# Output projection in two halves of three fp32r matmuls, query projections in parts, and low parts made on GpSimd

## What is computed

```
qn = layernorm(x, ln_q_g, ln_q_b)
q = qn @ Wq * scale                                   # 256x1024 for each batch
k, v = split(media @ Wkv)
sim = where(media_mask, q k^T, lowest);  attn = softmax(sim)
out = attn @ v                                        # 16 heads of 64 = 1024 columns
x = x + tanh(attn_gate) * (out @ Wo)                  # the output projection, Wo is 1024x256
x = x + tanh(ff_gate) * (gelu(layernorm(x) @ W1) @ W2)
... second layer: scores against media, softmax, context, gate, rmsnorm
```

## Time and profile before

| | |
|---|---|
| median of 3 runs | 854.41 us (853.79 to 854.54) |
| the profiled execution | 853.74 us, of which 851.9 us is the span from first to last instruction |
| TensorE busy | 821.6 us, 96% of the span |
| VectorE, ScalarE, GpSimd busy | 616.6, 466.6 and 420.4 us |
| mean granted TensorE clock | 0.996 of full speed |
| DMA | 16.81 MB, under a tenth of the time of the queues after the first slices |

### The profile page before, as it was taken

The page is one execution under the profiler, slowest core; times in us unless marked ns, Lnnn a source line. Parts: engine busy times, 40 slices in busy tenths (PEclk is TensorE's granted clock), DMA queues, the critical chain, the costliest instruction groups (busy, mean ns, idle before and its releaser), DMA issues.

```text
span 851.9 us, 18557 instructions
## 1 busy us (share of the span) xinstructions
PE 821.6 (96%) x7905; PEld 696.2 (82%) x7905; DVE 616.6 (72%) x996; ACT 466.6 (55%) x743; POOL 420.4 (49%) x205
## 2 busy tenths in 40 slices
PE   4999999999999999999999999999999989999996
PEld 3787888888888888888888888888888868998885
DVE  7856789867757898678478986784888766446385
ACT  5755665657536656576266565663555563126262
POOL 2445565655625656556355565564767686000002
PEclk9999999999999999999999999999999999999999
DMA  8100001000000010000000000000100502000001
GB/s 283 31 2 2 2 2 40 2 2 2 2 1 2 1 40 2 2 2 2 1 1 2 2 2 2 2 2 2 50 2 2 156 16 76 3 2 1 1 1 49
DMA packets 20560, 16.81 MB, mean 20 GB/s; under 512 B 1008, under 2 KB 19456, under 8 KB 20480
## 3 DMA queue, kind: packets, MB, share of 16 engines
q1 hardware_dynamic: 20192, 15.38, 6.1%
q10 hardware_dynamic: 288, 0.27, 0.1%
HBM read 14.59 MB, written 1.05 MB: 18 GB/s over the span
## 4 chain that ended last, share of the span: by engine, by line
PE 81%; DVE 11%; ACT 4%; POOL 2%; issue 1%; DMA 1%; ACTq 0%; POOLq 0%; DVEq 0%
PE psum L1396 22%; PE psum L382 18%; PE psum L1410 16%; PE psum L1365 7%; PE psum L1321 4%; PE psum L1425 3%; PE psum L1178 3%; PE psum L1260 2%; DVE mx L983 2%; DVE k_lo L972 2%; DVE ot L1013 2%; PE psum L1416 1%; ACT v L666 1%; POOL acc L495 1%; ACT k_hi L660 1%
## 5 line engine op out<-in xcount | busy, mean ns | idle before, releaser
L495 POOL TENSOR_TENSOR acc<-acc,ring 128x1024 f32<-128x1024 f32 x128 | 306.7, 2396 | 18.7 <-POOL acc L490 0.5
L983 DVE TENSOR_REDUCE mx<-psum 128x2 f32<-128x800 f32 (+2 forms) x256 | 245.3, 990 | 80.9 <-PE psum L1365 68.9
L683 ACT ACTIVATE ring<-psum 128x1024 f32<-128x1024 f32 x192 | 196.8, 1026 | 65.0 <-PE psum L1396 58.6
L490 POOL TENSOR_TENSOR acc<-ring 128x1024 f32<-128x1024 f32 x32 | 76.6, 2394 | 250.2 <-ACT ring L683 250.2
L1410 PE MATMUL psum<-ring,v 128*64 128x256 f32 (+1 forms) x1664 | 186.7, 381 | 1.8
L1410 PEld LDWEIGHTS psum<-ring,v 128*64 128x64 f32 (+1 forms) x1664 | 116.7, 137 | 60.6 <-DVE k_lo L972 3.9
L1396 PE MATMUL psum<-nm,maskrow 64*128 64x256 f32 (+1 forms) x832 | 124.4, 294 | 0.6 <-ACT ring L683 0.6
L1396 PE MATMUL psum<-q_hi,k_hi 64*128 64x256 f32 (+1 forms) x832 | 117.8, 278 | 0.0
L1396 PE MATMUL psum<-q_lo,k_hi 64*128 64x256 f32 (+1 forms) x832 | 117.6, 277 | 0.0
L1396 PE MATMUL psum<-q_hi,k_lo 64*128 64x256 f32 (+1 forms) x832 | 117.4, 277 | 0.0
L675 ACT COPY od<-psum 128x512 f32<-128x512 f32 x32 | 18.8, 587 | 153.2 <-PE psum L1416 153.2
(11 more groups left out here) (165 smaller groups left out, 1478.2 us busy)
## 6 DMA issues: line engine op xcount, KB each, us to landing
nat<-in_ctx_dram SPq DMA_DIRECT2D x7, 768.0 KB
w<-in_L_xattn_W_dram SPq DMA_DIRECT2D x2, 1024.0 KB, 6.4
wo<-in_L_xattn_Wo_dram SPq DMA_DIRECT2D x1, 1024.0 KB, 9.7
out_dram<-t_res SPq DMA_DIRECT2D x8, 128.0 KB, 1.7
mask<-in_mask_BxS_bk_dram SPq DMA_DIRECT2D x4, 200.1 KB, 7.0
nat<-in_ctx_dram SPq DMA_DIRECT2D x2, 384.0 KB, 7.4
ring<-in_L_xattn_Wkv_dram SPq DMA_DIRECT2D x2, 384.0 KB, 6.2
wq<-in_L_xattn_Wq_dram SPq DMA_DIRECT2D x1, 768.0 KB, 6.7
```

What stands on the lines that cost most here:

```text
L490: nc.gpsimd.tensor_tensor(acc[:, :, :, :], ring[:, 0, :, :, :], ring[:, 1, :, :, :], ALU.add)\
L495: nc.gpsimd.tensor_tensor(acc[:, :, :, :], acc[:, :, :, :], ring[:, g, :, :, :], ALU.add)\
L683: nc.scalar.activation(ring[:, g, :, :, :], score_set[m % 2].rearrange("p (h i q) -> p h i q", h=2, i=2), ACT.Exp).then_inc(S["p_ready"], 1)
L983: nc.vector.tensor_reduce(mx[:, t, :, c], pair[:, :, 0:min(c1, KEYS) - c0], axis=AX.X, op=ALU.max).then_inc(S["m_max"], 1)
```

## The change

1. The output projection O becomes two items, `("O", b, 0)` for pairs 0 to 3 and `("O", b, 1)` for pairs 4 to 7. The first stands in stage 5, the second where O stood. Each of its 8 products is three fp32r matmuls (high by high, high by low, low by high). H is also two items. The second H adds to what the first wrote.
2. `F` multiplies in place into `rec` (`ot_made`); a new item f on ScalarE rounds it to `ot_hi`, and GpSimd subtracts to get `ot_lo` (`output_lo`), which raises `ot_ready`. `rec` and `nm` now lie in parts of `ring` that the last group of keys leaves unused.
3. GpSimd splits `Wo` behind its sums of pairs 0 and 1 of batch 0, and `Wq` behind those of pairs 2 and 3.
4. From batch 1 on, G is three fp32r matmuls for each product, on `wq_hi`, `wq_lo`, `zt_hi`, `zt_lo`. A new item a (stage 5) makes `zt_hi` on ScalarE and `zt_lo` on VectorE.
5. `mt_lo` of the next batch moves from VectorE (item P) to GpSimd (`next_media_lo`, behind the sums of pair 5). Two of the four Y move from stage 4 to stage 5.
6. The mask has one buffer instead of four and is loaded by SyncE for each batch; `unread` is gone.

```diff
-FULL_EXTRAS = {2: "G.3 Q.3", 3: "T.1.0 T.1.1 T.1.2", 4: "T.1.3 T.1.4", 5: "W.1", 6: "G.4 Q.4", 7: "G.5 Q.5", 9: "O.0 H.0 G.6 Q.6"}
-COLUMN_EXTRAS = {2: "B.1 J.1", 3: "c.1.0 c.1.1 c.1.2 X.1", 4: "c.1.3 c.1.4 Z.1 C.1 Y.1.0 Y.1.1 Y.1.2 Y.1.3", 5: "P.1.0 P.1.1 P.1.2 P.1.3", 7: "I.1.0 I.1.1"}
+FULL_EXTRAS = {2: "G.3 Q.3", 3: "T.1.0 T.1.1 T.1.2", 4: "T.1.3 T.1.4", 5: "O.0.0 H.0.0 W.1", 6: "G.4 Q.4", 7: "G.5 Q.5", 9: "O.0.1 H.0.1 G.6 Q.6"}
+COLUMN_EXTRAS = {2: "B.1 J.1", 3: "c.1.0 c.1.1 c.1.2 X.1", 4: "c.1.3 c.1.4 Z.1 C.1 Y.1.0 Y.1.1", 5: "a.1 Y.1.2 Y.1.3 P.1.0 P.1.1 P.1.2 P.1.3", 7: "I.1.0 I.1.1"}
...
-    return [("U", j)] + items(COLUMN_EXTRAS.get(j, "")) + [("A", j), ("D", j)]
+    return [("U", j), ("f", j - 1)] + items(COLUMN_EXTRAS.get(j, "")) + [("A", j), ("D", j)]
...
-                n += 2 if item[0] == "M" else 1
+                n += 2 if item[0] == "M" else ABANKS if item == ("O", 0, 0) else 1
...
+            def output_lo(b, n):
+
+                upto(pool, "ot_hi", b, n + 1)
+                nc.gpsimd.tensor_tensor(ot_lo[:, n % HALF, :], rec, ot_hi[:, n % HALF, :].bitcast(F32), ALU.subtract)\
+                    .then_inc(S["ot_ready"], 1)
...
+            def next_media_lo(b):
+
+                upto(pool, "mt_mixed", b, 2 * NCH)
+                for c, (c0, c1) in enumerate(REAL_CHUNKS):
+                    upto(pool, "mt_hi", b, NCH + c + 1)
+                    nc.gpsimd.tensor_tensor(mt_lo[:, c0:c1], mt[:, c0:c1], mt_hi[:, c0:c1].bitcast(F32), ALU.subtract)\
+                        .then_inc(S["mt_lo"], 1)
...
+                    if b or j:
+                        upto(pool, "acc_ready", b, j + 1)
+                        output_lo(b, j - 1)
+                    if b == 0 and j < 2:
+                        upto(pool, "acc_ready", b, j + 1)
+                        split_output_weights((2 * j, 2 * j + 1))
+                    if b == 0 and j in (2, 3):
+                        upto(pool, "acc_ready", b, j + 1)
+                        split_query_weights((0, 1) if j == 2 else (2, 3))
+                    if next_batch and j == 5:
+                        next_media_lo(b)
...
             sums(BATCH - 1, False)
+            output_lo(BATCH - 1, PAIRS - 1)
...
+            def output_hi(b, n):
+
+                upto(act, "ot_made", b, n + 1)
+                if n >= HALF:
+                    upto(act, "o_full", b, n // HALF)
+                nc.scalar.copy(ot_hi[:, n % HALF, :], rec).then_inc(S["ot_hi"], 1)
...
                     elif kind == "F":
                         upto(dve, "rec_ready", b, (n + 1) * RECIPROCAL_PARTS)
-                        if n == PAIRS:
-                            upto(dve, "o_full", b, 1)
-                        nc.vector.tensor_tensor(ot[:, n % PAIRS, :], od[:, 0:TOK], rec[:, :], ALU.mult)\
-                            .then_inc(S["ot_ready"], 1)
+                        nc.vector.tensor_tensor(rec, od[:, 0:TOK], rec, ALU.mult).then_inc(S["ot_made"], 1)
...
+                            parts = [(w[:, t, c], z_t[:, t, :]) for t in range(DT)
+                                     for w, z_t in (((wq_hi, zt_hi), (wq_lo, zt_hi), (wq_hi, zt_lo)) if in_parts else
+                                                    ((wq, zt),))]
...
+                        i0 = HALF * item[2]
+                        upto(pe, "ot_ready", b, i0 + HALF - 1)
                         for t in range(QT):
...
+                            q = slice(t * P, (t + 1) * P)
+                            for i in range(HALF):
+                                if t == 0 and i == HALF - 1:
+                                    upto(pe, "ot_ready", b, i0 + HALF)
+                                for k, (o, w) in enumerate(((ot_hi, wo_hi), (ot_hi, wo_lo), (ot_lo, wo_hi))):
+                                    last = mm(bank[:, t * DIM:(t + 1) * DIM], o[:, i, q], w[:, i0 + i, :],
+                                              start=(i == k == 0), stop=(i == HALF - 1 and k == 2))
                         last.then_inc(S["o_full"], 1)
```

More of the change, by code:

```diff
@@ L74, in first_order @@
 def first_order(body):
-    ahead = [i for i in body if i[1] >= AHEAD[i[0]]]
+    ahead = [i for i in body if i[1] >= AHEAD[i[0]] and i[0] != "a"]
     early = items("""X.1 B.1 T.1.0 c.1.0 T.1.1 c.1.1 T.1.2 c.1.2 T.1.3 c.1.3 Z.1 T.1.4 c.1.4 W.1 J.1 C.1 Y.1.0 Y.1.1 P.1.0 Y.1.2 P.1.1 Y.1.3 P.1.2 P.1.3 G.4
@@ L115, in cross_attention_kernel @@
     LAST = [k for i in BODY if i[1] < AHEAD[i[0]] for k in [i] + items(LAST_EXTRAS.get(i, ""))]
-    assert sorted(FIRST) == sorted(i for i in BODY if i[1] >= AHEAD[i[0]])
+    assert sorted(FIRST) == sorted(i for i in BODY if i[1] >= AHEAD[i[0]] and i[0] != "a")
     USES_BANK = "TWGKVRAOM"
@@ L255, in cross_attention_kernel @@
         KB = 1024
+        nm = at(starts["ring"] + 4 * ((GROUPS - 1) * 4 + 3) * TOK, "nm", [P, TOK], F32R)
+        wo_lo = at(starts["wo"], "wo_lo", [P, PAIRS, DIM], F32R)
+        wq_lo = at(starts["wq"], "wq_lo", [P, DT, INNER], F32R)
+        zt_hi, zt_lo = at(starts["z"], "zt_hi", [P, DT, TOK], F32R), at(starts["zt"], "zt_lo", [P, DT, TOK], F32R)
         MT_SIZE = 4 * KPAD + 24
@@ L956, in attention @@
                                                        ALU.mult, ALU.add).then_inc(S["mt_mixed"], 1)
-                    elif kind == "P":
+                    elif kind == "P" and order is FIRST:
                         c0, c1 = REAL_CHUNKS[item[2]]
@@ L961, in attention @@
                                                 ALU.subtract).then_inc(S["mt_lo"], 1)
+                    elif kind == "a":
+                        upto(dve, "zt_hi", b, n)
+                        nc.vector.tensor_tensor(zt_lo[:, :, :], zt[:, :, :], zt_hi[:, :, :].bitcast(F32), ALU.subtract)\
+                            .then_inc(S["zt_lo"], 1)
                     elif kind == "Q":
@@ L1316, in attention @@
                             pe.wait_ge(S["wq_in", n - PAIRS // 2], 16)
-                        upto(pe, "zt_in", b, n // (PAIRS // 2) + 1)
-                        for i in range(2):
-                            c0 = (2 * n + i) % PAIRS * P
-                            for t in range(DT):
-                                last = mm(bank[:, i * TOK:(i + 1) * TOK], wq[:, t, c0:c0 + P], zt[:, t, :],
-                                          start=(t == 0), stop=(t == DT - 1))
+                        in_parts = b * (PAIRS // 2) + n >= PAIRS // 2
+                        if in_parts:
+                            pe.wait_ge(S["wq_split"], 4)
+                            upto(pe, "zt_lo", b, n // (PAIRS // 2))
+                        else:
+                            pe.wait_ge(S["zt_in"], 1)
+                        for i in range(2):
+                            c = slice((2 * n + i) % PAIRS * P, ((2 * n + i) % PAIRS + 1) * P)
+                            parts = [(w[:, t, c], z_t[:, t, :]) for t in range(DT)
+                                     for w, z_t in (((wq_hi, zt_hi), (wq_lo, zt_hi), (wq_hi, zt_lo)) if in_parts else
+                                                    ((wq, zt),))]
+                            last = split_mm(bank[:, i * TOK:(i + 1) * TOK], parts)
                         last.then_inc(S["g_full"], 1)
@@ L1419, in attention @@
                     elif kind == "O":
-                        if order is LAST:
+                        if order is LAST and item[2]:
                             pe.wait_ge(S["ff_gelu"], 1)
-                        upto(pe, "ot_ready", b, PAIRS)
+                        if b == 0:
+                            pe.wait_ge(S["wo_split"], 4)
+                        i0 = HALF * item[2]
+                        upto(pe, "ot_ready", b, i0 + HALF - 1)
                         for t in range(QT):
-                            for i in range(PAIRS):
-                                last = mm(bank[:, t * DIM:(t + 1) * DIM], ot[:, i, t * P:(t + 1) * P], wo[:, i, :],
-                                          start=(i == 0), stop=(i == PAIRS - 1))
+                            q = slice(t * P, (t + 1) * P)
[5 more added lines that the diff above has]
+                                              start=(i == k == 0), stop=(i == HALF - 1 and k == 2))
                         last.then_inc(S["o_full"], 1)
```

93 lines of the change are left out of this document (59 added, 34 removed).

## The result

The changed kernel takes 849.39 us (median of 4 runs, 848.82 to 849.50) against 854.47 us (4 runs, 853.79 to 854.65): ratio 0.9941, 95% interval 0.9928 to 0.9953, faster by 5.1 us. The prediction was 849.8 us, range 846.5 to 853.8. The profiled execution's span is 847.0 us, before 851.9.

What follows compares the result with a forecast made beforehand. The prediction took TensorE's start-to-start matmul distances to bound the kernel through most of its span. Terms -5.2 - 3.6 + 4.6 - 2.3 + 0.5 + 1.45 = -4.55 us gave a median of 849.8 us, range 846.5 to 853.8.

Steps and rivals of the forecast that it cites:

- O, -5.2 us: Output projection as three fp32r matmuls a product, 0.12 us each: 5.7 instead of 7.0 us a batch, -5.2 us in four.
- G, -3.6 us: Query projections of batches 1 to 3 in three parts: 1.44 instead of 1.75 us, twelve times, -3.6 us.
- The wait behind O's first half, +4.6 us: In stage 5 W (in LAST a K) waits 1.15 us for the bank H reads; four batches, +4.6 us, bounds +3.6 to +6.
- M waits gone, -2.3 us: Stages 5 and 6: M waits vanish as Y and P move and TensorE arrives later; -2.3 us, bounds -2.4 and 0.
- GpSimd and VectorE, +0.5 us, all in batch 0: GpSimd's new work delays only small VectorE instructions of the column parts through the shared port: +0.5 us, bounds 0 and +3.
- The end, +1.45 us: In the last O TensorE waits for pair 7's low part after 9 matmuls: +1.45 us, bounds 0.9 and 2.5.
- The sum: All terms together: -4.55 us on the profiled execution's 853.74 us, giving 849.2, as a median 849.8 us, 0.5% faster.
- The two halves of O by themselves bring nothing.: Output projection: what three parts save, the bank wait takes; only G and VectorE's relief are left.
- GpSimd in stage 5: Low part 0.7 us, a wait for Y, media pieces 4.4, ending 6.5 to 7 us behind `acc_ready`, with some 7.5 free.
- this danger on instructions with two SBUF inputs: Shared read port: VectorE instructions with two SBUF inputs, as F (2.48 us against 0.42), block against GpSimd; `tensor_reduce` never does.

## Why the prediction was right, step by step

- **O, -5.2 us.** The mechanism is right, the size 0.5 to 0.9 us too large. 0.12 us from start to start is what the trace has, but one O of before took 7.01 us and the two halves take 2.98 and 2.96, 1.07 us less for a batch (4.3 in four) and not 1.3: each half starts with a distance of 0.22 us instead of 0.12, which the sum left out. When O is taken back it costs 4.4 us (4.7 by the distances of the D and of the end).
- **G, -3.6 us.** Right: 0.28 to 0.35 us in each of twelve places, 3.8 by their sum.
- **The wait behind O's first half, +4.6 us.** 1.13 us four times, 4.5. The reading from H's row of before, 1.15 us, was right to 0.02. The experiments add that the wait was avoidable, but not by the bank alone.
- **M waits gone, -2.3 us.** The size is right, the reasons only in part. Splitting Y gives 1.7 us. The wait of stage 6 went too, but not for P on GpSimd, which I named first: with P back on VectorE no M of stage 6 waited. What the prediction put beside it, TensorE's later arrival, is what remains; that it suffices follows from that run, that it is needed was not tested.
- **GpSimd and VectorE, +0.5 us, all in batch 0.** Mis-sized, within its bounds: from D to D the first four pairs take what they took before, so the term is 0. Three times the new low part cost 0.9 us in batch 0.
- **The end, +1.45 us.** 1.33: 1.45 us between the starts at 719.37 and 720.82 instead of 0.12. These are the rows of the changed kernel:

```profile
719.37 0.28 PE L1505 MATMUL psum<-wo_hi,ot_lo 128*128 128x256 f32 x1
720.82 0.39 PE L1505 MATMUL psum<-wo_hi,ot_hi 128*128 128x256 f32 x1 [1.17 <-POOL ot_lo L502]
```

```profile
718.62 1.03 ACT L596 ACTIVATE t_gelu<-psum 128x1024 f32<-128x1024 f32 x1 [0.92 <-PE psum L386]
719.54 0.40 ACT L669 CAST ot_hi<-ring 128x256 fp32r<-128x256 f32 x1
```

```profile
720.01 0.75 POOL L502 TENSOR_TENSOR ot_lo<-ring,ot_hi 128x256 fp32r<-128x256 f32 x1 [1.21 <-ACT ot_hi L669]
```

- **The sum.** -4.55 forecast, -4.9 from span to span, -5.1 between the medians. That it came out within 0.5 us is partly luck: O brought 0.5 to 0.9 us less than its term, and the 0.5 us for batch 0 that were never paid, with 0.1 to 0.2 us each at G, the wait and the end, made up for it.
- **"The two halves of O by themselves bring nothing."** Wrong by 1.8 us: they hide ScalarE's late `od` in stage 6. All the same they do not pay: their waits cost 4.5 us and the one in the last O 1.3, and O undivided was 3.9 us faster.
- **GpSimd in stage 5.** The low part took 2.20 us there and not 0.7, beside VectorE, and yet all was done at 167.4; the next sum, at 168.23, waited for ScalarE:

```profile
161.15 2.20 POOL L502 TENSOR_TENSOR ot_lo<-ring,ot_hi 128x256 fp32r<-128x256 f32 x1 [3.88 <-DVE acc L1068]
163.32 4.04 POOL L519 TENSOR_TENSOR mt_lo<-mt,mt_hi 128x402 fp32r<-128x402 f32 x4
168.23 2.40 POOL L528 TENSOR_TENSOR acc<-ring 128x1024 f32<-128x1024 f32 x1 [0.87 <-ACT ring L745]
```

## What to carry to other kernels

Where TensorE sets the time, price matmuls by the distance between starts of the same form in the trace, the first distance of a group by itself, and look at once for the bank of what is moved: who reads it before, who after, and what TensorE does meanwhile. An item that leaves a PSUM bank to a slower reader wants other items on both sides; another bank by itself only exchanges the reader that is waited for. When several edits go together, take them back one by one: here one (P on GpSimd) gave nothing, and one (half of O moved) hid a wait that another had made. And when TensorE's longest wait grows, read the granted clock behind it too: 5.2 us more of waiting cost 7.7.

## What the runs showed of the hardware that was not expected

A VectorE instruction of 0.23 us can become one of 2.46 us, and this decides 1.3 us of the kernel's time. `negl`, a `tensor_scalar` of 128x128 from SBUF to SBUF, takes 0.23 us in its 33 places of the first profiled execution of the changed kernel (0.28 in one). In the first repetition of the same kernel two of the 33 took 2.46. VectorE's, GpSimd's and TensorE's timelines there, GpSimd's from the second of its four additions on:

```profile
386.36 0.17 DVE L1054 TENSOR_REDUCE m<-mx 128x4 f32<-128x16 f32 x1
386.57 2.46 DVE L1059 TENSOR_SCALAR negl<-m 128x128 fp32r<-128x128 f32 x1
388.95 0.56 DVE L1039 TENSOR_TENSOR k_lo<-psum,k_hi 128x402 fp32r<-128x402 f32 x1
```

```profile
386.56 2.39 POOL L533 TENSOR_TENSOR acc<-acc,ring 128x1024 f32<-128x1024 f32 x1
```

```profile
389.57 0.45 PE L386 MATMUL psum<-mt_hi,wk_hi 128*128 128x400 f32 x1 [1.06 <-DVE k_lo L1039]
```

`negl` lasts as long as the addition, `k_lo` comes late, and a K waits for its bank. The same place in the first execution of the changed kernel, VectorE and GpSimd:

```profile
385.55 0.23 DVE L1059 TENSOR_SCALAR negl<-m 128x128 fp32r<-128x128 f32 x1
```

```profile
385.58 2.46 POOL L533 TENSOR_TENSOR acc<-acc,ring 128x1024 f32<-128x1024 f32 x1
```

There `negl` starts 0.03 us ahead of the addition, here 0.01 us behind its start. That is the whole difference, and it holds in all 13 profiled executions of this document, before included. Of their 429 `negl`, 26 start at least 0.008 us behind the start of one of GpSimd's additions and before its end: every one of these ends 0.08 to 0.09 us after the addition does, whatever is left of it, from 0.28 us for one that starts near its end to 2.47 for one that starts with it. The other 403 start between two additions, or with GpSimd idle, or within 0.004 us of an addition's start, and take 0.23 us at most, 377 of them so shortly before an addition or so close to its start that they run on into it. So a `negl` that starts behind the addition waits until the addition is done, and one that starts ahead of it does not.

The long ones of 2.4 us were 0, 2 and 1 in the three executions of the changed kernel, 1 with another bank, 1 with O behind W, 1 with P on VectorE and 0 in the other kernels, all in stage 8, each with 1.3 us more in that stage (1.5 with P on VectorE). With O undivided three `negl` of stage 6 took 0.52 us, and in the run with the tripled low part four took 0.71 to 0.99 and one 1.66, and no K waited. The kernel's text does not decide it, since the same kernel had 0, 2 and 1; some 0.01 us between two engines do. Spans of single executions were therefore not compared without taking these out. The start has to be taken out too: the first D comes anywhere from 55.4 to 57.1 us, and in the changed kernel alone at 55.87, 56.92 and 55.46. The stage lengths from D to D above are of stages without either.

The prediction had put this danger on instructions with two SBUF inputs, as F, and held the others safe; `negl` has one tensor input, so that ground was too weak. The Trainium skill (SBUF — State Buffer, Who interferes with whom) lists copy, cast and `tensor_scalar` as well, in the modes in which they use both ports, with the lock held for a whole instruction by whoever issues first; that `negl` ends 0.08 us behind the addition that started before it, and runs its 0.23 us when it starts first, agrees with that. What shifts the two engines against each other by 0.01 us from one execution to the next is open.
